# A six-part decoder on one core: weight loads regrouped and reordered, the last feed-forward cut into halves of 512 columns

## The reference, cut to what matters

```
x = LN(x + x + causal_attention(LN(x)))      # station a, "front", first part
x = LN(x + long_convolution(x, ctx))         # station a, "front", second part (the taps)
x = LN(x + ternary_ffn(x))                   # station c: weights tanh-rounded from w1, w2, w3, rows g1, g2, g3
x = LN(x + recurrent(x))                     # station c: Wr, Wk, Wv, Wo and the row "decay"
x = LN(x + cross_attention(x, ctx))          # stations k, q, x, y, o: 16 heads, 4 key heads
x = LN(x + ffn(x))                           # station a, "ffn": fp8 operands, bf16 results
# ffn: gate = gelu(bf16(x8 @ Wg)); value = bf16(x8 @ Wu); out = bf16(fp8(gate * value) @ Wl), 256 -> 1024 -> 256
```

## Time and profile before

| | us |
|---|---|
| median of three runs | 837.78 |
| the profiled execution, its own time | 837.24 |
| its span, first to last instruction | 835.2 |
| PE busy | 796.5 (95%) |
| DVE busy | 650.1 (78%) |
| ACT busy | 528.7 (63%) |
| POOL busy | 335.6 (40%) |

### The profile page before, as it was taken

One profiled execution on the slowest core, in us unless ns is written; L12 is line 12 of the kernel. 1 busy time (PEld: TensorE's weight loads), 2 busy tenths in 40 slices (PEclk: granted clock), 3 DMA queues, 4 the chain that ended last, 5 costly groups with the idle time before them and its releaser, 6 DMA issues.

```text
span 835.2 us, 13794 instructions
## 1 busy us (share of the span) xinstructions
PE 796.5 (95%) x4554; PEld 610.9 (73%) x4554; DVE 650.1 (78%) x1696; ACT 528.7 (63%) x1315; POOL 335.6 (40%) x419
## 2 busy tenths in 40 slices
PE   6899998899999999999999999999999999999985
PEld 5564576688878777886788767887788778777763
DVE  1678778798889787988878987898879877755655
ACT  3776732773664697538863598359854588578763
POOL 0686875354256213632525313723543242112110
PEclk9999999999999999999999999999999999999998
DMA  9977311001003000200100010100110001000000
GB/s 323 344 250 249 91 64 26 0 14 26 1 2 86 4 2 0 77 0 2 38 13 17 10 60 8 62 1 0 40 51 1 1 1 51 1 13 2 1 13 25
DMA packets 40517, 41.20 MB, mean 49 GB/s; under 512 B 19072, under 2 KB 34944, under 8 KB 40064
## 3 DMA queue, kind: packets, MB, share of 16 engines
q1 hardware_dynamic: 40448, 40.33, 15.2%
HBM read 31.93 MB, written 8.39 MB: 48 GB/s over the span
## 4 chain that ended last, share of the span: by engine, by line
PE 76%; DVE 10%; ACT 7%; issue 2%; POOL 2%; DMA 1%; SPq 0%; POOLq 0%; DVEq 0%; ACTq 0%
PE bank L1376 11%; PE bank L1337 10%; PE bank L1103 6%; PE bank L1160 6%; PE bank L1355 6%; PE bank L1365 5%; PE bank L1297 5%; PE bank L1230 3%; PE bank L1161 3%; PE bank L1190 3%; PE bank L1360 3%; PE bank L1097 2%; PE bank L1343 2%; PE bank L1243 2%; PE bank L1204 2%
## 5 line engine op out<-in xcount | busy, mean ns | idle before, releaser
L1337 PE MATMUL bank<-XTE,w_xq 128*128 128x256 f32 x512 | 122.0, 381 | 2.6 <-ACT QA L721 2.1
L729 ACT ACTIVATE S<-S,mx 128x128 f32<-128x128 f32 x256 | 99.4, 394 | 28.3 <-DVE mx L1034 28.0
L1376 PE MATMUL bank<-w_xo,OX 128*128 128x256 f32 x512 | 115.9, 379 | 0.0
L1337 PEld LDWEIGHTS bank<-XTE,w_xq 128*128 128x128 f32 x512 | 94.4, 190 | 20.4 <-issue 4.3
L1376 PEld LDWEIGHTS bank<-w_xo,OX 128*128 128x128 f32 x512 | 95.3, 190 | 12.2 <-issue 0.2
L1031 DVE SCALAR_TENSOR_TENSOR S<-bank,rq,xmask 128x128 f32<-128x128 f32 x256 | 71.6, 342 | 23.9 <-PE bank L1355 19.9
L720 ACT ACTIVATE QS<-bank,per_partition_sb 128x256 f32<-128x256 f32 x128 | 60.9, 475 | 28.4 <-PE bank L1337 28.2
L1160 PE MATMUL bank<-prod,taps_sb 128*128 128x256 f32 x256 | 77.6, 385 | 0.3 <-DVE Zc L846 0.3
L1355 PEld LDWEIGHTS bank<-KTX,QA 128*128 128x128 f32 x512 | 62.7, 191 | 11.5 <-issue 7.5
L1355 PE MATMUL bank<-KTX,QA 128*128 128x128 f32 x512 | 67.8, 279 | 2.2 <-ACT QA L721 1.7
L315 POOL TENSOR_TENSOR prod<-XTA,ccolA 128x256 f32<-128x256 f32 x96 | 59.1, 648 | 25.4 <-DVE prod L315 14.4
(11 more groups left out here) (230 smaller groups left out, 1744.3 us busy)
## 6 DMA issues: line engine op xcount, KB each, us to landing
keys_spilled<-KTX SPq DMA_DIRECT2D x6, 512.0 KB, 2.9
values_spilled<-VX SPq DMA_DIRECT2D x6, 512.0 KB, 4.1
KTX<-keys_spilled SPq DMA_DIRECT2D x6, 512.0 KB, 3.8
VX<-values_spilled SPq DMA_DIRECT2D x6, 512.0 KB, 4.7
xin<-in_x SPq DMA_DIRECT2D x8, 256.0 KB, 3.0
taps_sb<-in_taps SPq DMA_DIRECT2D x1, 2048.0 KB, 13.4
cnat<-in_ctx SPq DMA_DIRECT2D x8, 256.0 KB, 2.8
ccolA<-in_ctxT SPq DMA_DIRECT2D x32, 64.0 KB, 2.7
```

Source lines behind the costliest of these rows:

```text
L729: ins = nc.scalar.activation(S[:, b, seq(h)], S[:, b, seq(h)], ACT.Exp, bias=mx[:, b, h:h + 1], accum_out=sm[:, b, h:h + 1])
L1337: ins = nc.tensor.matmul(cols(EQ)[:, h], w_xq[:, k, hh * XDIM:(hh + 1) * XDIM], XTE[:, k], start=k == 0, stop=k == HALVES - 1)
L1376: ins = nc.tensor.matmul(rows(EY)[:, b], OX[:, h, b], w_xo[:, n * XGROUP + h], start=n == 0 and h == 0 and b == 0, stop=n == XKV - 1 and h ...
```

## The change

It has three parts.

First, the loads. The steps of SP's set_up that held several loads are cut: same_head and taps are a step of their own (letter b), decay and the rows g1, g2, g3 another (g), and w_rkv, w_o1 and upto a third (d). decay is now counted with the rows (group "c", four loads), same_head and taps alone in "b". By the new string SP issues: identity and w_qkv; context 0; group a; x of group 0; context 1; key weights; w1T; w2T; cnat and ccolA of group 0; same_head and taps; w3T; decay and the rows; context 2; query and output weights; context 3; spill 0; x of group 1; context 4; gate weights; up weights; spill 1; lin weights; and w_rkv with its two companions between context 6 and spill 3.

Second, the last feed-forward (group 7) has programs of its own on ACT, DVE and PE (`last_ffn`). Each of the four halves of 512 columns goes by itself through product, four transposes (into its own gate bank), a copy to fp8 of 512 columns, and four of the eight matmuls of its sequence. The gate half j = 3 is copied by DVE instead of ACT. The normalising of group 6 (`normalised(6)`) is put behind the four products on DVE.

Third, the strings of ORDER are new for every engine. In PE's, the sum of the second ternary weight (abs, i = 1) stands ahead of the convolution's skip matmul, and the four projections of key step 1 stand ahead of the convolution's step 1; in ACT's, the copy of the gate weights stands ahead of the second copy of transposed keys of step 1; in DVE's, the copy of the turned w_k stands ahead of the first norm, and in the feed-forward of group 6 both products stand ahead of the cross attention's sum (L1044); in PE's, the last convolution of group 1 stands between the two transposes of key step 7. The strings of PE, DVE, ACT and POOL differ in many other places, mostly by exchanges of neighbours; ACT's keep the number of changes between its tables. They are left out below.

```diff
--- before.py
+++ after.py
...
-        for_group = {"0": 2, "a": 3, "b": 3, "c": 3, "d": 3, "e": 4, "f": 2}
+        for_group = {"0": 2, "a": 3, "b": 2, "c": 4, "d": 3, "e": 4, "f": 2}
...
+        def last_half(k):
+
+            return (GROUPS - 1) * GB + k + 1
...
-        def station_a(front, ffn):
+        def station_a(front, ffn, last_ffn):
             for g in range(GROUPS):
                 yield from front(g)
                 if g >= AHEAD - 1:
                     yield from ffn(g - AHEAD + 1)
-            for g in range(GROUPS - AHEAD + 1, GROUPS):
+            for g in range(GROUPS - AHEAD + 1, GROUPS - 1):
                 yield from ffn(g)
+            yield from last_ffn(GROUPS - 1)
 
...
                 stage_load(0, "w1T")
+                yield
+                stage_load(1, "w2T")
+                yield
+                stage_load(2, "w3T")
+                for i, w in ((3, "gate"), (4, "up"), (5, "lin")):
+                    yield
+                    stage_load(i, w)
+
+            def convolution_loads():
+                yield
                 load("b", same_head[:], a["same_head"])
-                load("b", decay[:], a["L1_attn_decay"].partition_broadcast(P))
                 load("b", taps[:], a["taps"])
+
+            def row_loads():
+                yield
+                load("c", decay[:], a["L1_attn_decay"].partition_broadcast(P))
                 load("c", g12[:, 0], a["L0_ffn_g1"].partition_broadcast(P))
                 load("c", g12[:, 1], a["L0_ffn_g2"].partition_broadcast(P))
                 load("c", g3[:], a["L0_ffn_g3"].partition_broadcast(P))
-                yield
-                stage_load(1, "w2T")
+
+            def recurrent_weights():
+                yield
                 load("d", w_rkv[:], by_k(a["w_rkv"]))
                 load("d", w_o1[:], by_k(a["w_o1"]))
                 load("d", upto[:], a["upto"])
-                yield
-                stage_load(2, "w3T")
-                for i, w in ((3, "gate"), (4, "up"), (5, "lin")):
-                    yield
-                    stage_load(i, w)
 
...
-            together(ORDER["sp"], s=set_up(), w=keys_weights(), t=attention_weights(), a=each_group(front), k=keys(), v=reloads(), o=each_group(store))
+            together(ORDER["sp"], s=set_up(), w=keys_weights(), t=attention_weights(), b=convolution_loads(), g=row_loads(), d=recurrent_weights(), a=each_group(front), k=keys(), v=reloads(), o=each_group(store))
...
-                act.wait_ge(sems["loaded_b"], 16 * for_group["b"])
+                act.wait_ge(sems["loaded_c"], 16 * for_group["c"])
...
-                    if g == GROUPS - 1:
-                        act.wait_ge(sems["f_g16"], nth(g, 2 * GB, j))
-                        ins = nc.scalar.activation(half, half, ACT.Gelu_apprx_tanh)
-                        if nh == 1:
-                            sig(ins, "f_ga")
-                yield
-                for b in range(GB if g < GROUPS - 1 else 0):
+                yield
+                for b in range(GB):
                     act.wait_ge(sems["f_g16"], nth(g, 2 * GB, 2 * b + 1))
                     sig(nc.scalar.activation(G16[:, b], G16[:, b], ACT.Gelu_apprx_tanh), "f_ga")
                 for b in range(GB):
@@ -643,6 +654,36 @@
                     act.wait_ge(sems["f_aT"], nth(g, GB, b))
                     settled(act)
                     sig(nc.scalar.activation(A8T[:, b].rearrange("p k s -> p (k s)"), as_bf((A0, A1)[b]), ACT.Copy, saturate=False), "f_a8")
+
+            def last_ffn(g):
+                def gate(j):
+                    half = G16[:, j // 2, j % 2 * BANK:(j % 2 + 1) * BANK]
+                    if j < 3:
+                        act.wait_ge(sems["f_gf"], nth(g, 2 * GB, j))
+                        sig(nc.scalar.activation(half, ffn_banks(g, j)[0][:], ACT.Copy), "f_g16")
+                    act.wait_ge(sems["f_g16"], nth(g, 2 * GB, j))
+                    sig(nc.scalar.activation(half, half, ACT.Gelu_apprx_tanh), "f_ga")
+
+                def turned(j):
+                    b, nh = j // 2, j % 2
+                    act.wait_ge(sems["f_aT"], last_half(j))
+                    settled(act)
+                    sig(nc.scalar.activation(A8T[:, b, 4 * nh:4 * nh + 4].rearrange("p k s -> p (k s)"),
+                                             as_bf(ffn_banks(g, j)[0])[:, 0:BANK], ACT.Copy, saturate=False), "f_a8")
+                yield
+                act.wait_ge(sems["f_xT"], nth(g))
+                settled(act)
+                sig(nc.scalar.activation(X8[:], cols(turned_bank(g)), ACT.Copy, saturate=False), "f_x8")
+                for j in range(3):
+                    yield
+                    gate(j)
+                yield
+                turned(0)
+                yield
+                gate(3)
+                for j in range(1, 4):
+                    yield
+                    turned(j)
 
...
-                    if g == GROUPS - 1 and b == 0:
+                dve.wait_ge(sems["f_yu"], nth(g, GB, GB - 1))
+                norm("f", UA)
+                if g < GROUPS - 2:
+                    yield
+                    normalised(g)
+
+            def normalised(g):
+                dve.wait_ge(sems["nf_rstd"], nth(g))
+                norm_out("f", UA, X[g % XBUF])
+
+            def last_ffn(g):
+                x = X[g % XBUF]
+
+                def value(j):
+                    dve.wait_ge(sems["f_gf"], nth(g, 2 * GB, j))
+                    sig(nc.vector.tensor_copy(F16[:, j // 2, j % 2 * BANK:(j % 2 + 1) * BANK], ffn_banks(g, j)[1][:]), "f_f16")
+
+                def product(j):
+                    half = G16[:, j // 2, j % 2 * BANK:(j % 2 + 1) * BANK]
+                    dve.wait_ge(sems["f_f16"], nth(g, 2 * GB, j))
+                    dve.wait_ge(sems["f_ga"], last_half(j))
+                    sig(nc.vector.tensor_tensor(half, half, F16[:, j // 2, j % 2 * BANK:(j % 2 + 1) * BANK], ALU.mult), "f_a")
+                for j in range(2):
+                    yield
+                    value(j)
+                yield
+                product(0)
+                yield
+                value(2)
+                yield
+                product(1)
+                yield
+                dve.wait_ge(sems["f_gf"], nth(g, 2 * GB, 3))
+                dve.wait_ge(sems["f_g16"], nth(g, 2 * GB, 2))
+                sig(nc.vector.tensor_copy(G16[:, 1, BANK:2 * BANK], ffn_banks(g, 3)[0][:]), "f_g16")
+                yield
+                value(3)
+                for j in range(2, 4):
+                    yield
+                    product(j)
+                yield
+                normalised(g - 1)
+                for b in range(GB):
+                    yield
+                    dve.wait_ge(sems["f_y"], nth(g, GB, b))
+                    order(nc.vector.tensor_copy(Y16[:, b], ffn_banks(g, 2 * b)[1][:, 0:DIM]))
+                    sig(nc.vector.tensor_tensor(UA[:, b], x[:, b], Y16[:, b], ALU.add), "f_yu")
+                    if b == 0:
                         dve.wait_ge(sems["f_yu"], nth(g, GB, 0))
                         nc.vector.bn_stats(stats["g"][:, b], UA[:, b])
                 dve.wait_ge(sems["f_yu"], nth(g, GB, GB - 1))
-                norm("f", UA, GB - 1 if g == GROUPS - 1 else 0)
-                yield
-                dve.wait_ge(sems["nf_rstd"], nth(g))
-                norm_out("f", UA, x)
+                norm("f", UA, GB - 1)
+                yield
+                normalised(g)
 
...
+                if g == GROUPS - 1:
+                    return
...
+            def last_ffn(g):
+                yield from ffn(g)
+                def turned(j):
+                    b, nh = j // 2, j % 2
+                    pe.wait_ge(sems["f_a"], last_half(j))
+                    for k in range(4):
+                        ins = nc.tensor.transpose(as_bf(ffn_banks(g, j)[0])[:, seq(k)], G16[:, b, seq(4 * nh + k)], ident_bf[:])
+                    sig(ins, "f_aT")
+
+                def result(b):
+                    for nh in range(2):
+                        pe.wait_ge(sems["f_a8"], last_half(2 * b + nh))
+                        settled(pe)
+                        for k in range(4 * nh, 4 * nh + 4):
+                            ins = nc.tensor.matmul(ffn_banks(g, 2 * b)[1][:, 0:DIM], A8T[:, b, k], w_ln[:, k], start=k == 0, stop=k == FFN_K - 1)
+                    sig(ins, "f_y")
+                for j in range(3):
+                    yield
+                    turned(j)
+                yield
+                result(0)
+                yield
+                turned(3)
+                yield
+                result(1)
 
...
     "sp": (
-        "asskwsasksktkkskaskskkkkkkakaaaavaavoaoaaaovavoavvoooo"
+        "sksakwssabsgktkkaksskskkkdkkakkaaaaavaoaaoavaoavavovvoooo"
     ),
```

More of the change, by code:

```diff
@@ L379, in set_up @@
                     stage_load(i, w)
+            def convolution_loads():
+                yield
+                load("b", same_head[:], a["same_head"])
+                load("b", taps[:], a["taps"])
```

(13 more changed lines are left out.)

61 lines of the change are left out of this document (27 added, 34 removed).

## The result

The changed kernel takes 838.76 us (median of 20 runs, 837.07 to 841.85), the kernel before on the same chip 837.5 (20 runs): ratio 1.0019, 95% interval 1.0011 to 1.0027. By this ratio it is slower by 1.6 us (0.9 to 2.3), where 3.2 us less had been forecast. The profiled executions stand at 836.5 (span) and 838.60 (own time) against 835.2 and 837.24.

A forecast was written before the change was run, and what follows sets the result against it. The queue and the two last feed-forwards set the ends, PE's own work all between. Gains 0.5 + 0.3 + 1.2 + 1.2 = 3.2 us take the median from 837.78 to 834.6, range 831.5 to 838.9.

The forecast's parts named there:

- The start: PE's first work: w_qkv issued ahead of group 0's x lets PE start 0.5 us earlier, bounds 0.2 and 0.5.
- The taps: Taps loaded behind w2T and first contexts: land near 26.7, wanted at 31.0, 4 us of cover, cost 0.
- Up to 69 us: PE's restart after the spill 1 wait at 69.43: 0.5 us earlier taken, bounds 0.5 earlier to 0.7 later.
- The rows and w_rkv: Loads in the head moved behind others: wanted only after 65 and 110 us, so cost 0.
- Key step 7: A convolution step between its transposes hides PE's 0.34 us wait before 138.54: gain 0.3, between 0 and 0.6.
- The middle: 160 to 800 us: neighbours exchange but each engine's work is the same, cost 0; at most 7.9 us idle to gain.
- Rival 4: Middle exchanges put a late step ahead of ready ones; three waits of 1.73, 5.2 us, giving 839.8; chance 0.12.
- My own test: Sign for the middle: PE's idle time between 160 and 800 us stays within 2 us of 7.9.
- Group 6: Its feed-forward's second product ahead of the cross-attention sum starts group 7's block 1.2 us earlier; bounds 0.8 and 1.5.
- Group 7: Last feed-forward by halves: 7.4 instead of 8.6 us from first gate copy to last result copy, gain 1.2.
- Rival 3 (clock): Clock falls in the last block, slowing projections, last transposes and matmuls: 3.4 us, giving 838.0; chance 0.08.
- the head's gain of 0.8: Head in all: the start's 0.5 plus key step 7's 0.3, bounds +0.7 and -1.4.

The follow-up runs named there:

- e5: Changed kernel with w_rkv, w_o1 and upto issued behind spill 3 instead of ahead of it; ratio 1.0017 to the kernel before.
- e14: Kernel before with the changed end and one PE exchange at 489 us: transposes of Q4's rows ahead of the second ones of group 2's product; 834.69 us.
- e2: Kernel before with only the changed end: group 6's two products ahead of the cross-attention sum, group 7 by halves; 834.22 us, ratio 0.9965.
- e3: Changed kernel's loads and orders up to 150 us, the kernel before's orders behind, changed end; 835.48 us, ratio 0.9990.
- e11: Kernel before with the changed end, and spill 1 issued ahead of the up weights; 834.17 us, ratio 0.9952.
- e13: Kernel before with the changed end and one DVE step moved at 496 us: softmax scaling ahead of a squared gate and a normalising; 835.50 us.
- e10: As e3, but w_rkv and companions issued behind spill 3, query and output weights behind spill 5; 834.41 us, ratio 0.9954 to the kernel before.
- e12: Head edits of e10 and e11 together, the kernel before's middle orders, changed end; 836.45 us, ratio 0.9984.
- e16: As e12, with the gate weights right behind spill 0 and the changed orders in 150 to 390 us; 834.72 us, ratio 0.9976.
- e6: As e3, with the query and output weights, then w_rkv and companions, issued behind spill 5; 848.65 us, ratio 1.0137.
- after: The changed kernel itself, all parts of the change together, against the kernel before; 838.76 us, ratio 1.0019.
- e4: Kernel before's loads and orders up to 150 us, the changed kernel's orders behind, changed end; 837.79 us, ratio 1.0010.
- e15: As e11, with the changed kernel's orders in 150 to 390 us; 834.89 us, ratio 0.9976.

## Why the prediction was wrong

*The start:* forecast 0.5, measured 1.8 (7.45 to 5.64). The size was off. w_qkv is issued 0.55 us earlier, as I counted, but also lands sooner after its issue, 4.4 us for 5.7. That the bytes of x no longer go ahead of it is the likely reason. Part of the 1.8 is luck: PE starts at 6.72 to 7.55 in the eleven profiles with the old loads and at 5.48 to 6.29 in the eight with the new ones, 1.5 apart on average. 0.4 of it is back at 20 us, since x lands later than before (8.38 us for 3.64), DVE's first norm starts only then, and PE waits 1.17 us for its result. *The taps:* forecast to land near 26.7, landed at 27.2, and nobody waited.

*Up to 69 us:* "PE goes on 0.5 us earlier". It went on at 68.83 for 69.43, 0.6. The number is right, the reason half: the gate load is at 52.49 (53.7 forecast) and PE waits 1.16 us for the copy behind spill 1, but the lead of 2.8 us at 50 was down to 0.4 at 60 already, taken by spill 0 behind the 4 MB. That order is the kernel before's; I had not asked how early spill 0 can land. In my rows' trace it landed 2.35 us ahead of ACT's copy, so a lead beyond that was lost from the start.

*"The rows and w_rkv are wanted after 65 and 110 us; cost 0":* wrong. I asked when the loads are wanted, not what stands behind them. Spill 3 does. It costs 1.4 us in place (e5), of which the times show no more than 0.2. *Key step 7:* 0.3 forecast, the place moves 0.2 between 100 and 150.

*"The middle. ... Cost 0":* the step that failed most, 3.4 us. Rival 4 named the mechanism, but with three waits of 1.73 us, to be seen as PE's idle time grown beyond 11.1 us. Idle time grew by 0.46; the loss is in short waits that the idle time mostly does not show, and e14 shows one exchange making one. Which exchanges make up the rest stays open. My own test ("PE idle within 2 us of 7.9") came out as forecast while 2.7 us were lost between 160 and 800: it was no test. My other premise, that exchanges of neighbours leave the work the same, is true and beside the point.

*Group 6:* forecast 1.2, measured 1.4. From G6 to ACT's first gate copy 8.91 us before (811.28 to 820.19), 7.47 after. *Group 7:* forecast 7.4 from that copy to DVE's last result copy, measured 830.06 - 822.39 = 7.67; gain 0.9 for 1.2. Together 2.3 for 2.4: right in this profile, where 814 to 818 and the projections behind it are at full clock. *Rival 3 (clock)* did not come in this profile, and that is in part luck. In five others with the same end (e2, e3, e5, e11, e13) group 7's sixteen projection matmuls take 5.30 us instead of 3.61, and in e2 the span pays 1.4 us of the 3.4 that I had priced. The 20 executions of the changed kernel fall in two halves: ten at a mean clock of 0.998 or 0.999 with a median of 838.1, ten at 0.994 to 0.997 with 839.9. Where the clock fell in those was not recorded.

Sum of what was measured in the profiles: head +0.3, middle +3.4, end -2.3: +1.4; the spans differ by 1.3. The forecast had -0.8, 0 and -2.4. So the step that failed is the middle at cost 0, and behind it the head's gain of 0.8.

## What to carry to other kernels

Ask of a load that moves not only when it is wanted but which small transfer the queue puts behind it, and who waits for that one; bulk goes behind the spills that free buffers. In a stretch where the engine is 99% busy an exchange of neighbours is not free: count instructions per window rather than idle time, and try such a list by stretches, for here two of three stretches held the loss. A lead won in front is worth what the next load-bound wait leaves of it, so mend that wait first: e11, with the old head and one letter of SP's string moved, is as fast as e10 with its whole new head (0.9952 and 0.9954). When an end is short of work, look at the clock in several executions before its gain is counted.

## What the runs showed of the hardware

The clock is granted at its lower level (1.2 GHz) for a part of 70 to 74 us in some profiles only, behind PE's wait for the value copy and eight transposes: 0.65 of full in e10, 0.57 in e3, 0.72 in e12 as a mean over the 4 us, and the 16 matmuls of key step 4 then take 8.80 us (e10) instead of 7.11 (e5). The size of the wait does not decide it: 2.07 us in e3 and 1.51 in e10 with, 2.27 in e16 and 1.45 in e6 without. The Trainium skill, TensorE: Matmul & The Clock Gate, Part 4: PE-mode transpose, says that transposes do not count as activity in the way matmuls do; e10 agrees, and e16, with the same eight transposes at full clock, shows that they are not enough by themselves. It is why single places behind 70 us differ by 1.5 to 2 us between kernels with the same list (e3 stands at +2.5 at 100 us, after at +0.5).

The same holds at the end: e2 and e14 have the same lists behind 492 us, and between 818 and 822 us the clock is 0.65 of full in e2 and 1.00 in e14. What decides it no run here shows.

The kernels with the old head differ in place at 20 us by up to 1.9 us (e4 -1.59, e15 +0.28) and keep most of that to the end. So an edit of 1 us is read from the change of place behind it, not from one time.
